# A graph recommender on one core: one-hots six tiles ahead, six PSUM banks for sums, no product wait in the gather queue

## The reference, cut to what matters

```python
N, DIM, N_EDGES, LAYERS = 12501, 128, 150000, 2
h = acc = emb                                    # (N, 128) fp32
for _ in range(LAYERS):
    h = segment_sum(adj_val[:, None] * h[adj_col], adj_row, num_segments=N)
    acc = acc + h
graph = acc / (LAYERS + 1)
combined = graph[items] + item_features[items]   # 512 sessions of 50 items
...                                              # two small dense layers and a weighted sum per session
scores = select @ l2norm(graph).T                # (512, 12501)
```

## Time and profile before

| what | value |
|---|---|
| median of 3 runs | 4893.78 us |
| profiled execution, its own time | 4908.07 us |
| its span | 4906.3 us |
| mean granted TensorE clock | 0.729 of full speed |
| TensorE busy | 2961.6 us, 60% |
| VectorE busy | 2994.3 us, 61% |
| GpSimd busy | 2963.5 us, 60% |
| ScalarE busy | 871.1 us, 18% |

### The profile page before, as it was taken

One profiled execution on the slowest core, in us unless ns is written; L12 is line 12 of the kernel. 1 busy time (PEld: TensorE's weight loads), 2 busy tenths in 40 slices (PEclk: granted clock), 3 DMA queues, 4 the chain that ended last, 5 costly groups with the idle time before them and its releaser, 6 DMA issues.

```text
span 4906.3 us, 44211 instructions
## 1 busy us (share of the span) xinstructions
PE 2961.6 (60%) x9770; PEld 1792.5 (37%) x9770; DVE 2994.3 (61%) x7246; ACT 871.1 (18%) x3004; POOL 2963.5 (60%) x3059
## 2 busy tenths in 40 slices
PE   4888884555555555555555555555555555554688
PEld 2777772232332323322323323332332333222344
DVE  8999984555555555555555555555555555555455
ACT  1999881000000000000000000000000000004443
POOL 1566666665666666666664666666666666664650
PEclk8888886666667676667766777777677767776789
DMA  0000001111111111111114111111111111133363
GB/s 30 3 3 3 3 3 46 43 46 42 45 44 46 44 46 44 44 44 44 46 43 137 45 46 46 44 46 46 44 46 45 45 45 46 45 96 84 43 113 140
DMA packets 140023, 234.88 MB, mean 48 GB/s; under 512 B 56500, under 2 KB 84080, under 8 KB 139760
## 3 DMA queue, kind: packets, MB, share of 16 engines
q0 software_dynamic: 95904, 177.31, 15.5%
q1 hardware_dynamic: 41476, 55.61, 3.4%
q10 hardware_dynamic: 2508, 0.60, 0.1%
HBM read 192.37 MB, written 41.01 MB: 48 GB/s over the span
## 4 chain that ended last, share of the span: by engine, by line
DVE 33%; another core or an unknown queue 31%; issue 21%; PE 8%; ACT 3%; DVEq 3%; POOL 1%; DMA 1%; ACTq 0%; SPq 0%; POOLq 0%
DVE acc L1086 19%; DVE ring L1037 5%; ACT big L592 2%; PE bank L1438 2%; DVEq L1076 2%; PE bank L1362 1%; DVE stage L873 1%; PE bank L1299 1%; PE bank L1466 1%; DVE big L817 1%; DVE ring L825 1%; DVE junkl L1058 1%; PE bank L1425 1%; POOL sorted_edges L492 1%
## 5 line engine op out<-in xcount | busy, mean ns | idle before, releaser
L1362 PE MATMUL bank<-ring 128*128 128x256 f32 x4968 | 2007.8, 532 | 1642.1 <-DVE ring L1037 1066.5
L1362 PEld LDWEIGHTS bank<-ring 128*128 128x128 f32 x4968 | 1081.7, 250 | 2548.0 <-DVE ring L1037 1525.9
L1086 DVE TENSOR_TENSOR acc<-acc,bank 128x256 f32 x2484 | 1020.0, 411 | 1498.7 <-remote 1243.2
L522 POOL DMA_INDIRECT ring<-in_L_rec_emb,cring x1242 | 1174.6, 946 | 664.9 <-issue 355.3
L522 POOL DMA_INDIRECT ring<-table,cring x1242 | 1172.6, 944 | 663.1 <-issue 352.8
L1037 DVE TENSOR_SCALAR ring<-bank,mlo,mval 128x256 f32<-128x256 f32 x2484 | 1330.2, 536 | 11.7 <-DMA ring<-table,cring 11.2
L608 ACT COPY mlo<-ring 128x24 f32 (+1 forms) x104 | 22.0, 211 | 3422.9 <-PE bank L1362 2428.4
L592 ACT ACTIVATE big<-big 128x68 f32<-128x68 bf16 x1764 | 559.1, 406 | 5.7 <-issue 5.6
L1299 PE MATMUL bank<-big,ring 128*128 128x136 f32 x2352 | 440.3, 333 | 87.3 <-issue 24.8
L492 POOL DMA_INDIRECT sorted_edges<-moved,block_to x313 | 386.8, 1236 | 102.3 <-issue 101.7
L1299 PEld LDWEIGHTS bank<-big,ring 128*128 128x128 f32 x2352 | 366.8, 225 | 158.6 <-ACT big L592 83.9
(11 more groups left out here) (209 smaller groups left out, 1615.5 us busy)
## 6 DMA issues: line engine op xcount, KB each, us to landing
scores<-stage SPq DMA_DIRECT2D x48, 512.0 KB
ring<-in_L_rec_emb,cring POOLq DMA_INDIRECT x1242
ring<-table,cring POOLq DMA_INDIRECT x1242
table<-big SPq DMA_DIRECT2D x7, 896.0 KB, 8.1
combined<-ring SPq DMA_DIRECT2D x7, 896.0 KB, 7.4
sorted_edges<-moved,block_to POOLq DMA_INDIRECT x313
ring<-combined,sidi POOLq DMA_INDIRECT x200
sorted_edges<-ring SPq DMA_DIRECT2D x1, 1248.0 KB, 4.4
```

The source lines that it names most:

```text
L522: pool.indirect_dma_start(msg[:, s, :], None, source, bass.IndirectOffsetOnAxis(cring[:, s:s + 1], 0)).then_inc(s_g[s], 16)
L1086: add = dve.tensor_tensor(acc[:, bass.ds(off, BUCKET)], acc[:, bass.ds(off, BUCKET)], bank[u % PR][:, 0:BUCKET], ALU.add)
L1362: pe.matmul(bank[u % PR][:, 0:BUCKET], msg[:, h * T + u, :], onehot[:, u % SR, :], start=True, stop=True).then_inc(s_mm[u % M], 1)
```

## The change

One-hots are built six tiles ahead instead of four, into six buffers instead of eight. The sums go round six PSUM banks (0 to 5) instead of four (0 to 3). The transposed embeddings of layer 1, which used banks 5 and 6 in turn, use bank 6 alone, so that TensorE now waits for the add of the block just before. GpSimd's wait for the product 12 tiles back, before each eighth gather, is taken out; what is left is the wait for ScalarE's index copies at each step of 24.

```diff
-    SR, PR, LEAD = 8, 4, 4
-    PACE, AHEAD = 8, 12
+    SR, PR, LEAD = 6, 6, 6
@@ gather_step
                 for u in range(tiles_of(c)):
                     s = h * T + u
-                    if u % PACE == 0:
-                        done = NU * layer + T * c + u - AHEAD
-                        if done > 0:
-                            pool.wait_ge(s_mm[(done - 1) % M], (done - 1) // M + 1)
                     pool.indirect_dma_start(msg[:, s, :], None, source,
@@ add_embeddings
                 dve.tensor_tensor(acc[:, bass.ds(2 * D * c, 2 * D)], acc[:, bass.ds(2 * D * c, 2 * D)],
-                                  bank[5 + h][:, 0:2 * D], ALU.add).then_inc(s_ea, 1)
+                                  bank[6][:, 0:2 * D], ALU.add).then_inc(s_ea, 1)
@@ transpose_embeddings
                 pe.wait_ge(s_ec, c + 1)
-                pe.wait_ge(s_ea, c + 1)
+                pe.wait_ge(s_ea, c + 2)
                 for q in range(2):
-                    last = pe.transpose(bank[5 + h][:, q * D:(q + 1) * D], gnr[:, h, q, :], ident[:, :])
+                    last = pe.transpose(bank[6][:, q * D:(q + 1) * D], gnr[:, h, q, :], ident[:, :])
```

## The result

The changed kernel takes 5038.51 us (median of 4 runs, 5031.24 to 5045.83), the kernel before beside it 4896.43 us (4 runs, 4873.68 to 4899.33). The ratio is 1.030, with a 95% interval of 1.027 to 1.034: **slower by 3%**. The forecast was 5155 us.

The account below looks back on a forecast made before the run. No engine was full; late sums while gathers run held VectorE's adds. Cycles of 37.5 us add 261 us to the profiled execution, 5169, less 14 for the median: 5155 us, range 4750 to 5380.

Parts of the forecast that it names:

- four marks: Signs of being right: late adds 3.5 to 5 us apart, GpSimd pausing at step starts, recovery 3 us later, over 1498.7 us idle.
- 36.2 to 39.4: Bounds in us on one 24-tile cycle in the gather layers, making +126 to +457 us, 5020 to 5350 in all.
- With fewer pauses, more of each cycle is slow: Gather layers: one GpSimd pause per 24 gathers instead of one per 16 or 24 lengthens the slow share; +261 us.
- Sums 4.2 us apart: Mean spacing of late sums at VectorE's adds in slow stretches; bounds 3.5 to 4.9 us.
- Asked for later than 8.3 us after a restart is late: Onset of late sums after GpSimd resumes gathers; VectorE, six tiles ahead, stays quick 3.0 us more.
- A slow stretch of 21.4 us with 5.1 tiles: Late part of each 24-tile cycle, 32.7 - 11.3 us, at 4.2 us a tile.
- Step start +2.2: Extra us per cycle at a step's start: 3.04 us between two adds instead of 0.785.
- 37.5 us a step, +112 and +149: Chosen cycle time between 36.9 and 38.4 us; 51.75 steps make 1941 us a layer, against 1829 and 1792.
- The embeddings in bank 6 alone, at no cost: TensorE's wait for the previous block's add is covered by a step of over 30 us; uncovered, 20 us.
- TensorE recovers by itself, and gathers set the pace: Rival for the layers: gathers alone at 1.25 us a tile, 1565 us a layer, 4403 us in all; 6%.
- The lead rival: Sums turn late when gathers are few tiles ahead, not after 8 us of running; 1689 us a layer, 4651 us; 12%.

Follow-up runs that it names:

- Q: Condition, not a fixed chip property, without late sums: the kernel before took 4286 to 4294 us in five of nine follow-up comparisons; the changed kernel's ratio was 1.0010.
- L: Condition with late sums: the kernel before took 4902 to 4918 us in four of nine follow-up comparisons; the first comparison, ratio 1.030, was made under it.

## Why the prediction came out as it did

**Right in sign, pattern and range.** All four marks held: adds 3.5 to 5 us apart (up to 5.6) in stretches of about 20 us, once per step; GpSimd pauses of some 6.8 us at step starts only; the last long gap ending about 3 us into the pause; more idle time before the adds. A step takes 36.4 us, inside the 36.2 to 39.4 given.

**Its reason holds only in part.** "With fewer pauses, more of each cycle is slow" did not come true: slow stretches hold 51% of each layer in both kernels. The loss lies inside them, where a tile now takes 4.6 us instead of 3.9 and 4.2, and, in layer 1, in step starts that they no longer cover. The prediction took the spacing of late sums as a constant, 4.2 us, whatever the run of gathers.

**Mis-sized, with errors that cancel in part.**
- *Sums 4.2 us apart* in slow stretches: measured 4.9 to 5.6 for most, 4.6 a tile over the whole stretch. The 4.2 came from one stretch of the earlier trace rows cut short by a pause.
- *Asked for later than 8.3 us after a restart is late*, so the last quick add at 11.3: measured 14.7 (mean over 100 restarts; in the cycle above, 24 gathers before the pause, GpSimd restarted at 1484.18, and 1497.94 is 13.8 later). The two stretches that I read follow pauses of 3.3 and 3.85 us. After the 113 pauses of 3 to 4 us in the kernel before, the last quick add comes 11.0 us after the restart, and after its 19 pauses of over 5 us 13.2 us: after a longer pause the sums stay quick for longer. The changed kernel has only long ones, and two further tiles ahead make 13.2 into 14.8.
- *A slow stretch of 21.4 us with 5.1 tiles*: measured 18.7 with 4. *Step start +2.2*: measured 2.8 and 2.7 us between the two adds, so +2.0.
- *37.5 us a step, +112 and +149*: 36.4, and +56 and +86. That is the whole miss of 116 us.
- *The embeddings in bank 6 alone, at no cost*: so it was. VectorE's add of them, which waited 62.3 us before, waits for nothing now.

**Wrong: the ground it stood on.** I wrote that this case's trace disagrees with the Trainium skill's rule (page "SBUF — State Buffer", section "Who interferes with whom") that DMA never contends with a compute engine. The run with plain DMAs, 76 GB/s without a late sum, agrees with the rule as far as traffic goes; a pause that ends late sums did not show that traffic makes them. The extra small DMAs beside gathers, which lengthened the slow stretches from 19.3 to 23.4 us, are the one case here in which other DMAs mattered.

**Missed: that all this depends on a condition outside the kernel.** The rival "TensorE recovers by itself, and gathers set the pace" (4403 us, 6%) describes what both kernels do under Q, 1540 us a layer where it had 1565. Nothing in one profile could give that a chance; a missing landing time in the DMA issues was the one sign that something was odd.

**The lead rival fell:** nearly all slow stretches begin with GpSimd 22 or 23 tiles ahead.

**What stays open.** What an indirect gather does, under L, that holds back a product's signal. The runs leave: it is bound to the indirect instruction and not to its addresses or its bytes (all gathers here had 128 pieces; their number was not varied); it builds up over 11 to 15 us, drains in 3 to 4, and small DMAs add to it. At its end all outstanding products signal 40 ns apart in the trace (before, from 1061.21 on), though their matmuls had started long before. Under L the trace also lacks update records wherever indirect DMAs run: up to 150 us, when the first stage issues its first one, it holds as many as under Q (588 and 587), and from there to 740 us 2,870 where the run under Q holds 6,817.

The Trainium skill's page "NOTIFIC — the notification-queue block", section "Overflow: three behaviours, one of which stalls the engine", says that this block's inner pipeline holds back its producers and does not lose a record, and that stalls counted there would mean an engine throttled by it. The trace agrees in that late signals and lost records come with the same instructions. By the page, though, a lost record is the work of a full ring in memory, which is another case. No run here put this to the test. Every run here, under L and Q, was recorded, so whether sums are late at all in a run without a trace is open as well.

## What to carry to other kernels

A wait in a gather queue can be a pause that something else needs: before taking it out, look at what ends with it. When one engine's results come late in bursts, run the kernel before again on other occasions before tuning against it; here a 3% loss, and a 14% slower baseline, belonged to the occasion. And where gathers set the pace, 1.25 us a tile against 0.785, reordering the other engines was worth nothing.

## What was not expected of the hardware

- The same kernel on the same chip: 4902 and 4294 us on two occasions.
- An indirect gather of 128 rows keeps GpSimd 0.94 us, plus 0.30 to the next, whether rows are scattered, in a row, or 128 bytes long; a plain DMA of 128 rows 0.54 us on GpSimd and 0.47 on SyncE.
- Halving each product's columns dropped the granted clock in layer 1 from 0.72 to 0.50 of full speed and cost no time, since the layer was bound elsewhere.
- Under one condition a product's signal came up to 19 us after its matmuls had been started, while TensorE stood idle.
